# Graph layers on one core: chunks of target blocks cut as sixteen of three and one of one

## The chip, the cores and the metric

The kernel runs on one core of one Trainium2 chip. The metric is the device time of one execution in microseconds (us); the median of three runs stands for a kernel.

## What is computed

Four graph networks stand one behind another, on 6250 nodes with 128 features and 100000 edges, with a residual sum and a layer norm behind each. The first two are attention networks. The work that the change touches is the last two, which sum over neighbours, cut here to what matters:

```python
# third network: four graph convolutions (self-loops, degree norm)
h = relu(gcn_conv(x, edges, W1, b1)); h = relu(gcn_conv(h, edges, W2, b2))
h = relu(gcn_conv(h, edges, W3, b3)); h = relu(gcn_conv(h, edges, W4, b4))
x = layernorm(x + h)
# fourth network: two GIN convolutions on the same edges
def gin_conv(x, src, dst, Wa, ba, Wb, bb):
    h = x + segment_sum(x[src], dst)
    return relu(h @ Wa + ba) @ Wb + bb
h = relu(gin_conv(x, ..., W1a, b1a, W1b, b1b))     # 128 -> 256 -> 256
h = relu(gin_conv(h, ..., W2a, b2a, W2b, b2b))     # 256 -> 256 -> 128
x = layernorm(x + h)
```

## The kernel before

Nodes are padded to 49 blocks of 128. An earlier phase counts the edges between every pair of blocks into a dense matrix of bytes in HBM (`adjacency`). The phase `dense` (L2084) then computes a graph layer as a matrix product: the features of 49 source blocks, each split into a high and a low part that add up to it (`parts`, type fp32r), are the stationary operands, and the counts of a chunk of target blocks are the moving operand.

The phase runs seven units (`UNITS`): three of kind `gcn`, one `gcn_end`, and `gin`, `gin_left` and `gin_right` (the second GIN layer takes its 256 features in two halves). The function `chunks` (L2016) cuts the 49 target blocks of a unit into 17 chunks of up to three blocks (`TRIO`). Each pair of unit and chunk is an item, 7 x 17 = 119 in all. A chunk of n blocks is n*128 columns wide.

Within an item the 49 source blocks go by in 17 groups k of three (the last group has one). For each group one engine turns the bytes of the chunk into fp32r numbers in one of four buffers `moving`: the string `SHARES` says which, seven times GpSimd (L2229), six times ScalarE (L2350), four times VectorE (L2495). TensorE then issues two matmuls for each source block of the group (L2288), each with a weight load of its own, so 98 matmuls in an item whatever the width of the chunk, all adding up in one bank of PSUM. A cast may run up to four groups ahead of TensorE (it waits for `eaten` of the group four before).

What is to be done with an item's sums, its steps, is written into the next item: the functions `step` of TensorE (L2233), ScalarE (L2307) and VectorE (L2400) issue the steps of item g-1 at fixed groups k of item g. For `gcn` these are the product with the norm at k = 0, the relu at k = 2, the product with the next weights on TensorE at k = 4 (L2240), the product with the norm at k = 7, and the split into parts for the next layer (VectorE cuts and subtracts at k = 7 and 8, ScalarE copies at k = 10). `gcn_end` has transposes at k = 4 (L2245), row statistics at k = 7, the normalization, the cut and the low part at k = 12 and 13, the high part at k = 14. `gin` and `gin_right` have the hidden product at k = 2 (L2252, L2254, L2255) and the output product at k = 8 (L2263). The last item's steps come behind its matmuls with nothing beside them.

In the first item of a unit TensorE waits at each group for the parts of the chunk that holds the group's last source block (`holding`, L2124).

The counts of an item come by one DMA on SyncE's queue into one of two buffers (`load`, L2153). The load of item g waits until all casts of item g-2 are done. In program order SyncE goes through load(g), load_norm(g), store(g-3), load_x(g). VectorE's `fill(g+1)` (L2356) waits, behind k = 11 of item g, for the counts of item g+1 to land and adds the self-loops; all casts of item g+1 wait for that, and so do VectorE's own later steps and its cast k = 15 of item g, which stand behind it.

Of the kernel before, what the change touches and what calls it, by code (L numbers as in the profile page):

```python
# [24 lines left out]
P = 128  # L25
NODES, EDGES, D = 6250, 100000, 128
BLOCKS = -(-NODES // P)
# [369 lines left out]
def wait(engine, sem, n):  # L397

    if not (isinstance(n, int) and n <= 0):
        engine.wait_ge(sem, n)  # L400
# [1603 lines left out]
TRIO = 3  # L2004
# [10 lines left out]

def chunks():  # L2016

    pairs = -BLOCKS % TRIO
    sizes = [TRIO] * ((BLOCKS - 2 * pairs) // TRIO) + [2] * pairs
    assert sum(sizes) == BLOCKS  # L2020
    return [(sum(sizes[:k]), n) for k, n in enumerate(sizes)]


CUTS = len(chunks())
ITEMS = [(u, kind, b, n) for u, kind in enumerate(("first",) + UNITS) for b, n in chunks()]
SIGNALS = {"first": "cut high low",
           "gcn": "scaled relued projected rowed cut high low",
# [12 lines left out]
def upto(name, e):  # L2040

    return COUNT_TO[name, e] if e >= 0 else 0
# [41 lines left out]
def dense(nc, m, d, t, tables, adj, out):  # L2084
# [14 lines left out]
    with Phase(nc, "de", names) as (  # L2099
# [9 lines left out]
        def item(g):  # L2109
            u, kind, b, n = ITEMS[g + CUTS]  # L2110
            return u - 1, kind, b, n, g + CUTS
# [12 lines left out]
        def holding(block):  # L2124

            return [e for e, (b, n) in enumerate(chunks()) if b <= block < b + n][0]
# [8 lines left out]
        def normed(kind):  # L2135
            return kind in ("gcn", "gcn_end")
# [14 lines left out]
        @block.sync  # L2151
        def _(sp):
            def load(g):  # L2153
                u, kind, b, n, e = item(g)
                wait(sp, by_act, (g - 1) * SHARE["a"])
                wait(sp, by_dve, (g - 1) * SHARE["d"])
                wait(sp, by_pool, (g - 1) * SHARE["p"])
                sp.dma_start(d.counts[g % 2][:, 0:n * SLOTS * WIDE].rearrange("p (b w) -> p b w", b=n),
                             adj[b * P:(b + n) * P, :].rearrange("(b p) w -> p b w", p=P)).then_inc(counts_in[g % 2], 16)

            def load_norm(g):
                u, kind, b, n, e = item(g)
                if normed(kind):
                    wait(sp, scaled, upto("scaled", e - 2))
                    sp.dma_start(d.norm_row[g % 2][:, 0:n * P],
                                 tables["norm"].rearrange("(o b) p -> o (b p)", o=1)[:, b * P:(b + n) * P].broadcast_to([P, n * P])
                                 ).then_inc(norm_in[g % 2], 16)

            def load_x(g):
                u, kind, b, n, e = item(g)  # L2170
                if kind in ("gcn_end", "gin_right"):
                    wait(sp, rowed if kind == "gcn_end" else rested, upto("rowed" if kind == "gcn_end" else "rested", e - 2))
                    if kind == "gin_right":
                        sp.wait_ge(stored, 16 * CUTS)
                    sp.dma_start(d.x_in[g % 2][:, 0:n * P].rearrange("p (b f) -> p b f", f=P),
                                 tables["x1" if kind == "gcn_end" else "x"][b * P:(b + n) * P, :].rearrange("(b p) f -> p b f", p=P)
                                 ).then_inc(x_in[g % 2], 16)

            def store(g):
                if g < 0:  # L2180
                    return
                u, kind, b, n, e = item(g)
                if kind == "gcn_end":
                    sp.wait_ge(lned, upto("lned", e))
                    sp.dma_start(tables["x"][b * P:(b + n) * P, :].rearrange("(b p) f -> p b f", p=P),
                                 d.h[:, 0:n * P].rearrange("p (b f) -> p b f", f=P)).then_inc(stored, 16)
                if kind == "gin_right":
                    sp.wait_ge(lned, upto("lned", e))
                    whole_blocks = n if (b + n) * P <= NODES else n - 1
                    last = sp.dma_start(out[b * P:(b + whole_blocks) * P, :].rearrange("(b p) f -> p b f", p=P),  # L2190
                                        d.h[:, 0:whole_blocks * P].rearrange("p (b f) -> p b f", f=P)).then_inc(stored, 16)
                    if whole_blocks < n:
                        sp.dma_start(out[(b + n - 1) * P:NODES, :], d.h[0:LAST, (n - 1) * P:n * P]).then_inc(stored, 16)

            load(0)
            load(1)
            for k, name in enumerate(("g2", "g3", "g4")):
                r, c = t[name].shape
                sp.wait_ge(padded, 3)
                sp.dma_start(d.g[k][0:r, 0:c], t[name]).then_inc(params_in, 16)  # L2200
            sp.dma_start(d.w1a[:, :], t["w1a"]).then_inc(params_in, 16)
            for to, name in ((d.w1b, "w1b"), (d.w2a, "w2a"), (d.w2b, "w2b")):
                sp.dma_start(to, t[name].rearrange("(k p) n -> p k n", p=P)).then_inc(params_in, 16)
            spread_at = {name: sum(n for _, n in SPREAD[:k]) for k, (name, _) in enumerate(SPREAD)}
            for to, name, n in ((d.b1b, "b1b", 2 * D), (d.b2b, "b2b", D)):
                sp.dma_start(to[:, :], t["spread"][:, spread_at[name]:spread_at[name] + n].broadcast_to([P, n])).then_inc(params_in, 16)
            sp.wait_ge(norm_copied, 1)
            sp.dma_start(tables["norm"], d.a[0:BLOCKS, 0:P]).then_inc(norm_out, 16)
            sp.wait_ge(norm_out, 16)
            sp.wait_ge(low, upto("low", 1))  # L2210
            for g in range(total):
                if g >= 2:
                    load(g)
                load_norm(g)
                store(g - 3)
                load_x(g)
            for g in range(total - 3, total):
                store(g)
            sp.wait_ge(stored, 16 * (2 * CUTS + 1))

        @block.gpsimd
        def _(pool):
# [628 lines left out]
```

## Time and profile before

| | us |
|---|---|
| median of three runs | 5488.98 (5485.43 to 5491.85) |
| the profiled execution | 5493.95 |
| its span | 5492.1 |
| the dense phase in it | 3311.0 to 5492.1, of which TensorE is busy 2140.6 |

The granted TensorE clock over the whole span is 0.88 of full speed on average, 1.0 in nearly all of the dense phase. The profile's times are those of one execution, with what was busy on each engine, which wait ended the idle time before an instruction, and a chain of work followed back from the end. Matmuls overlap one another, so the price of one is read from the distance between starts in an undisturbed row, not from its duration.

### The profile page before, as it was taken

How to read it: one execution, taken by the hardware profiler on the slowest of the kernel's cores; microseconds unless marked ns; L12 is line 12 of the kernel's file. 1: busy time of each engine (PE TensorE's matmuls, PEld its weight loads, DVE VectorE, ACT ScalarE, POOL GpSimd, SP SyncE). 2: the span in 40 equal slices, each digit the busy share in tenths (PEclk: the TensorE clock that was granted, in tenths of full speed). 3: DMA queues.
4: the chain of work that ended last, by engine and by line, in shares of the span. 5: the costliest groups of instructions: out<-in, count | busy, mean ns of one | idle time of the engine just before them, and what ended most of it. 6: DMA issues, size and time to landing. Idle time of an engine off the chain costs nothing. (4 is left out here: it accounts for less than half of the span.)

```text
span 5492.1 us, 99934 instructions
## 1 busy us (share of the span) xinstructions
PE 4376.5 (80%) x24072; PEld 3667.3 (67%) x24073; DVE 3581.9 (65%) x7941; ACT 2266.5 (41%) x4134; POOL 2777.4 (51%) x2730
## 2 busy tenths in 40 slices
PE   7566667666567777777648848999999999999998
PEld 4455555554234444444347738999999999999998
DVE  4888888886478888888786675444445654443444
ACT  0333443332135555555426644444444443344333
POOL 0477777773047777777412103444444443344433
PEclk8788888887887777877779959999999999999999
DMA  1444444442157777777425534343434442233332
GB/s 46 121 117 117 118 117 116 117 116 81 33 168 198 198 200 197 199 198 198 136 65 158 154 84 163 141 151 143 149 141 161 173 151 106 101 135 144 138 125 94
DMA packets 543152, 750.77 MB, mean 137 GB/s; under 512 B 57967, under 2 KB 441966, under 8 KB 542734
## 3 DMA queue, kind: packets, MB, share of 16 engines
q1 hardware_dynamic: 461182, 521.35, 28.4%
q0 software_dynamic: 81552, 224.63, 15.4%
q8 instruction: 166, 2.72, 0.2%
q14 instruction: 252, 2.06, 0.1%
HBM read 584.36 MB, written 161.41 MB: 136 GB/s over the span
## 5 line engine op out<-in xcount | busy, mean ns | idle before, releaser
L544 POOL DMA_INDIRECT arena<-table_kv,arena x1664 | 1732.7, 1041 | 653.1 <-issue 505.2
L2288 PE MATMUL ps<-moving,parts 128*128 128x384 f32 (+1 forms) x11662 | 2015.8, 331 | 38.5 <-ACT moving L2350 20.4
L2288 PEld LDWEIGHTS ps<-moving,parts 128*128 128x128 f32 x11662 | 1949.5, 188 | 72.1 <-ACT moving L2350 29.3
L2229 POOL CAST moving<-counts 128x1152 fp32r<-128x1152 uint8 (+1 forms) x420 | 476.2, 1134 | 737.9 <-PE ps L2288 606.4
L340 ACT ACTIVATE counted<-ps 128x392 uint8<-128x392 f32 x1568 | 665.0, 503 | 333.7 <-PE ps L331 300.3
L2229 POOL CAST moving<-big 128x1152 fp32r<-128x1152 uint8 (+1 forms) x413 | 468.6, 1135 | 610.1 <-PE ps L2288 610.1
L331 PE MATMUL ps<-by_place,by_lo 128*128 128x392 bf16 x1568 | 631.2, 525 | 105.3 <-DVE by_place L295 74.2
L654 PE MATMUL ps<-arena 128*128 128x137 f32 x1664 | 321.3, 349 | 344.6 <-DVE arena L788 332.5
L2350 ACT ACTIVATE moving<-counts 128x1152 fp32r<-128x1152 uint8 (+1 forms) x360 | 366.9, 1024 | 436.0 <-PE ps L2288 433.0
L2350 ACT ACTIVATE moving<-big 128x1152 fp32r<-128x1152 uint8 (+1 forms) x354 | 360.4, 1023 | 429.7 <-PE ps L2288 429.6
L654 PEld LDWEIGHTS ps<-arena 128*128 128x128 f32 x1664 | 273.1, 239 | 374.0 <-ACT arena L699 222.5
L2495 DVE CAST moving<-counts 128x1152 fp32r<-128x1152 uint8 (+1 forms) x240 | 312.7, 1303 | 287.7 <-PE ps L2288 287.6
L2495 DVE CAST moving<-big 128x1152 fp32r<-128x1152 uint8 (+1 forms) x236 | 307.4, 1302 | 289.7 <-PE ps L2288 289.7
L562 PEld LDWEIGHTS ps<-arena 128*128 128x128 bf16 x1680 | 140.7, 122 | 519.2 <-DVE arena L556 437.0
L321 DVE TENSOR_TENSOR slots<-slots,counted 128x196 uint16 x1568 | 405.7, 259 | 96.8 <-DVE slots L321 48.1
L562 PE MATMUL ps<-arena 128*128 128x128 bf16 x1680 | 197.3, 249 | 268.7 <-DVE arena L556 262.4
L295 DVE TENSOR_TENSOR by_place<-count_fours,count_place 128x1568 bf16<-128x1568 f16 (+1 forms) x497 | 395.2, 795 | 0.0
L331 PEld LDWEIGHTS ps<-by_place,by_lo 128*128 128x128 bf16 x1568 | 187.9, 124 | 254.7 <-issue 183.8
L883 PE MATMUL ps<-big,arena 128*128 x1672 | 323.3, 356 | 0.4 <-ACT arena L909 0.4
L883 PEld LDWEIGHTS ps<-big,arena 128*128 128x128 f32 x1672 | 300.7, 263 | 27.2 <-issue 18.5
L666 PE MATMUL ps<-big,arena 128*128 x1680 | 289.4, 330 | 0.4 <-ACT arena L694 0.4
L704 ACT ACTIVATE arena<-arena 128x32 f32<-128x32 f32 x208 | 48.3, 232 | 582.6 <-DVE arena L781 582.6
(329 smaller groups left out, 5337.3 us busy)
## 6 DMA issues: line engine op xcount, KB each, us to landing
counts<-adjacency SPq DMA_DIRECT2D x53, 2352.0 KB, 8.5
big<-adjacency SPq DMA_DIRECT2D x52, 2352.0 KB, 8.6
adjacency<-slots SPq DMA_DIRECT2D x784, 98.0 KB
edge_values<-arena SPq DMA_DIRECT2D x208, 256.0 KB
arena<-edge_values SPq DMA_DIRECT2D x208, 256.0 KB, 3.3
arena<-table_kv,arena POOLq DMA_INDIRECT x1664
big<-table_norm SPq DMA_DIRECT2D x60, 192.0 KB, 5.7
big<-adjacency SPq DMA_DIRECT2D x7, 1568.0 KB, 6.6
```

What stands on the lines that cost most here:

```text
L295: return dve.tensor_tensor(ct.by_place[:, r % 2, n], ct.fours[:, n], copies(ct.place[:, ds(c * HALF, HALF)], 1, last - first), ALU.is_equal)
L321: dve.tensor_tensor(ct.slot_pairs[:, ds(to[k], WIDE // 2)], ct.slot_pairs[:, ds(of[k], WIDE // 2)], ct.counted_pairs[:, r % 2, k, :], ALU. ...
L331: pe.matmul(m.bank(bank, WIDE), ct.by_lo[:, r % 2, :, k], ct.by_place[:, r % 2, :, k], start=True, stop=True).then_inc(ct.product, 1)
L340: act.activation(ct.counted[:, r % 2, k, :], m.bank(bank, WIDE), ACT.Copy).then_inc(ct.moved, 1)
L544: pool.indirect_dma_start(m.ring4[r][:, k * 2 * D:(k + 1) * 2 * D], None, table, bass.IndirectOffsetOnAxis(m.src[:, j * HALF + k:j * HALF ...
L562: mm = pe.matmul(bank[:, k * P:(k + 1) * P], m.hit16[:, r, :, k], m.ident16, start=True, stop=True)
L654: mm = pe.matmul(summed(k), m.hit[:, r % 2, k, :], m.msg[:, r % 2, k, :], start=True, stop=True)
L883: mm = pe.matmul(m.bank(6 + h)[:, k * P:(k + 1) * P], m.hitT[:, h, k, :], m.q[:, ds(at[k] * D, D)], start=True, stop=True)
L2229: pool.tensor_copy(to, of).then_inc(by_pool, 1)
L2288: mm = pe.matmul(m.bank(g % 2, n * P), d.parts[SOURCE[u]][:, s + q, t_, :], moving[:, q * n * P:(q + 1) * n * P], start=(s + q == 0 and t_ ...
L2350: act.activation(to, of, ACT.Copy).then_inc(by_act, 1)
L2495: dve.tensor_copy(to, of).then_inc(by_dve, 1)
```

## The change

`chunks` gives sixteen chunks of three blocks and one of one in place of fifteen of three and two of two. The number of chunks stays 17. Two places follow from it: in `gin_right` the last chunk has only the last, partial block, so its store of whole blocks falls away and only the store of the 106 remaining rows is left; the wait at the end counts one transfer fewer.

```diff
 def chunks():
 
-    pairs = -BLOCKS % TRIO
-    sizes = [TRIO] * ((BLOCKS - 2 * pairs) // TRIO) + [2] * pairs
+    sizes = [TRIO] * (BLOCKS // TRIO) + [BLOCKS % TRIO]
     assert sum(sizes) == BLOCKS
     return [(sum(sizes[:k]), n) for k, n in enumerate(sizes)]
...
                     whole_blocks = n if (b + n) * P <= NODES else n - 1
-                    last = sp.dma_start(out[b * P:(b + whole_blocks) * P, :].rearrange("(b p) f -> p b f", p=P),
-                                        d.h[:, 0:whole_blocks * P].rearrange("p (b f) -> p b f", f=P)).then_inc(stored, 16)
+                    if whole_blocks > 0:
+                        sp.dma_start(out[b * P:(b + whole_blocks) * P, :].rearrange("(b p) f -> p b f", p=P),
+                                     d.h[:, 0:whole_blocks * P].rearrange("p (b f) -> p b f", f=P)).then_inc(stored, 16)
                     if whole_blocks < n:
                         sp.dma_start(out[(b + n - 1) * P:NODES, :], d.h[0:LAST, (n - 1) * P:n * P]).then_inc(stored, 16)
...
-            sp.wait_ge(stored, 16 * (2 * CUTS + 1))
+            sp.wait_ge(stored, 16 * 2 * CUTS)
```

## Rows read from the trace of the kernel before

**Rows 1.** The page: busy time, and the granted TensorE clock in 40 slices.
```profile
PE 4376.5 (80%) x24072; PEld 3667.3 (67%) x24073; DVE 3581.9 (65%) x7941; ACT 2266.5 (41%) x4134; POOL 2777.4 (51%) x2730
...
PEclk8788888887887777877779959999999999999999
```

**Rows 2.** Busy time in two of the units; the last line sums all seven.
```profile
core 0: us, PE busy (x) PEld busy (x) DVE busy (x) ACT busy (x) POOL busy (x), PEclk, DMA share, GB/s
3611.30:3903.00 291.70, 291.62 (x1766) 289.19 (x1765) 133.03 (x186) 121.97 (x137) 136.98 (x119) 1.00 0.40 147
...
4837.70:5120.80 283.10, 281.48 (x1681) 280.56 (x1680) 115.64 (x156) 119.78 (x140) 132.49 (x119) 1.00 0.39 141
...
sum 2181.10, PE 2140.61 PEld 2085.48 DVE 1036.46 ACT 876.15 POOL 943.49; mean PE 305.80 PEld 297.93 DVE 148.07 ACT 125.16 POOL 134.78
```

**Rows 3.** Chain that ended last: an undisturbed run in three-block items, one in two-block items.
```profile
4659.24 6.24 PE ps L2288 x36
...
4810.45 4.31 PE ps L2288 x36
```

**Rows 4.** TensorE in order of time at half clock: start, us, what, count; then the clock, and durations in ns.
```profile
3254.62 1.06 PE L1376 MATMUL ps<-ident,arena 128*128 128x128 f32 x4
3256.69 3.31 PE L1828 MATMUL ps<-w,arena 128*128 128x100 f32 x14 [1.01 <-ACT arena L1817]
...
3260.00:3268.00 8.00, 1.75 (x7) 1.35 (x7) 7.76 (x13) 3.72 (x9) 0.00 (x0) 0.50 0.32 91
...
L1828 PE MATMUL ps<-w,arena x98: 421/421/534, 3222.7 to 3292.4; 128*128 128x100 f32 x98
```

**Rows 5.** Lines L2288, L2240, L2245: count, duration in ns min/median/max, first and last start.
```profile
L2288 PEld LDWEIGHTS ps<-moving,parts x11662: 186/188/333, 3311.0 to 5476.6; 128*128 128x128 f32 x198
...
L2240 PEld LDWEIGHTS ps<-dense_g,dense_b x294: 187/192/192, 3342.2 to 4201.5; 128*128 128x128 f32 x147
L2240 PE MATMUL ps<-dense_g,dense_b x294: 272/275/275, 3342.3 to 4201.6; 128*128 128x128 f32 x147
...
L2245 PEld LDWEIGHTS ps<-ident,dense_b x49: 138/141/145, 4218.6 to 4489.6; 128*128 128x128 f32 x49
```

**Rows 6.** TensorE in order of time at full clock: one step's six records.
```profile
3573.68 0.83 PE L2240 MATMUL ps<-dense_g,dense_b 128*128 128x128 f32 x6
```

**Rows 7.** Casts by width: busy us, mean ns.
```profile
L2229 POOL CAST moving<-counts 128x1152 fp32r<-128x1152 uint8 x370 | 434.3, 1174 | 553.4 <-PE ps L2288 551.9 <-DVE big L2363 1.5
...
L2350 ACT ACTIVATE moving<-counts 128x384 fp32r<-128x384 uint8 x53 | 27.8, 524 | 79.5 <-PE ps L2288 79.5
```

**Rows 8.** End of `gcn_end` in order of time: TensorE, SyncE's queue, VectorE, TensorE.
```profile
4461.72 0.49 PE L2245 MATMUL ps<-ident,dense_b 128*128 128x128 f32 x3
4474.00 0.38 PE L2245 MATMUL ps<-ident,dense_b 128*128 128x128 f32 x2
...
4455.08 0.39 SPq L2158 DMA_DIRECT2D big<-adjacency  x1
4469.15 0.38 SPq L2158 DMA_DIRECT2D counts<-adjacency  x1
...
4465.23 1.34 DVE L2396 TENSOR_SCALAR dense_h<-big,dense_two,dense_inverse 128x128 f32<-128x128 f32 x3
4478.71 1.32 DVE L2363 TENSOR_TENSOR counts<-counts,dense_one 128x128 uint8<-128x128 uint8 x3 [1.91 <-DMA counts<-adjacency]
...
4481.11 1.25 DVE L2376 TENSOR_TENSOR parts<-dense_h,dense_cut 128x256 fp32r<-128x256 f32 x1
...
4483.28 6.47 PE L2288 MATMUL ps<-moving,parts 128*128 128x256 f32 x38 [1.71 <-DVE moving L2495]
```

**Rows 9.** Chain that ended last, behind the last matmul over the counts.
```profile
5477.05 0.39 ACT dense_a L2316
...
5477.48 0.70 PE ps L2254 x2
...
5480.15 1.14 PE ps L2263 x8
```

## The prediction

> **What bounds the kernel now.** I read the page first: TensorE is the busiest engine, and in the last 16 or so of the 40 slices its clock is full and it is busy nine tenths or more [rows 1]. Those slices are the dense phase, the only part the change touches. A table of busy time cut at the starts of its seven units shows how tight it is: in a `gcn` unit TensorE is busy 291.62 of 291.70 us, in `gin_left` 281.48 of 283.10, in all 2140.61 of 2181.10, while VectorE, ScalarE and GpSimd are each busy less than half [rows 2]. So a unit's time is the number of its matmuls times the distance between their starts, and the question is what that distance is for each width of chunk. Casts, steps and loads matter only where one of them comes late.
>
> The chain that ended last gives the two prices known. An undisturbed run of 36 matmuls lasts 6.24 us in a three-block item (384 columns) and 4.31 us in a two-block item (256 columns) [rows 3]: 0.1733 and 0.1197 us each. For one block (128 columns) there is no row.
>
> **Part 1, the matmuls.** An item issues 98 matmuls at any width, and there are 17 items in a unit before and after. So the change takes two items of 98 at 0.1197 us out of each unit and puts in 98 at 0.1733 and 98 at an unknown price p:
>
> per unit 98 x (0.1733 + p - 2 x 0.1197) = 98 x (p - 0.0661) us.
>
> The bounds of p: if columns alone count, p lies on the line through the two known prices, 0.1197 - (0.1733 - 0.1197) = 0.0661, and the change costs exactly nothing here. If a narrower matmul saves nothing, p = 0.1197 and a unit costs 98 x 0.0536 = 5.25 us more.
>
> What could keep p off the line is the weight load, since each matmul brings its own 128 columns of weights and these don't get narrower. Two rows at half clock (0.50) speak to this: four f32 records with 128 moving columns take 1.06 us, and fourteen with 100 moving columns 3.31 us [rows 4]. Take off the last one's duration (0.421 us for L1828 [rows 4]; I take the same for L1376) and divide by the remaining 3 and 13: 0.213 and 0.222 us. With 22% fewer columns the distance doesn't fall at all; so something that doesn't depend on the moving columns sets it, and the weights are the same 128 columns in both. At full clock that floor would be half, 0.107 to 0.111. At full clock six records with 128 moving columns take 0.83 us, of which the last one's 0.275 is its tail: (0.83 - 0.275) / 5 = 0.111 [rows 5, 6].
>
> Does the floor hold for L2288, whose type is fp32r and not f32? By duration its weight loads are the same kind: 188 ns median against 192 for the f32 loads of L2240, while the load in front of a transpose (L2245) takes 141 [rows 5]. I take p = 0.111, because the nearest row in width, clock and duration of the weight load gives that. Then a unit costs 98 x (0.111 - 0.0661) = 4.40 us more, seven units **30.8 us**.
>
> Here the Trainium skill states two rules that part company. TensorE: Matmul & The Clock Gate, section LDWEIGHTS (loading the stationary operand), gives a load P / 1.2 ns, 107 ns for 128 columns, whatever is moved; by that figure the estimate would be 98 x 7 x (0.107 - 0.0661) = 28 us. Its section Back-to-back issue gap gives N / 2.4 + 2.5 ns, so 56 ns at 128 columns; by that rule the change would be free, since the same columns and the same number of matmuls are issued. The rows at 384 and 256 columns lie 11 ns above the second rule, and the rows at half clock follow the first.
>
> **Part 2, the steps on TensorE.** The steps of a three-block and a one-block chunk together issue the same number of records per block, or the same columns, as those of two two-block chunks. The six records of L2240 belong to one three-block chunk, two a block [rows 6]. Cost nothing; no cover is needed, the work is the same.
>
> **Part 3, the casts.** In a one-block item a group lasts 6 x 0.111 = 0.67 us at the forecast price, against 0.72 in a two-block item. Casts shrink more: GpSimd takes 1.174 us for 1152 elements, and ScalarE's one-block casts of 384 take 0.524 [rows 7]; I take 0.55 for 384 on any engine. The busiest, GpSimd, has seven casts in an item: 3.9 of 10.9 us. TensorE covers them. Without that cover (p on the line, a group of 0.40 us) GpSimd would still need only 3.9 of 6.5 us. Cost nothing, or a few tenths per unit where a step sits in front of a cast.
>
> **Part 4, the load behind the short item.** The next unit's first chunk is loaded while the last, short item runs. At the end of `gcn_end` this is late today [rows 8]: SyncE issues the load at 4469.15; VectorE, stopped in `fill` behind k = 11, goes on at 4478.71, 9.56 us later; fill, normalization, cut and low part stand in front of its cast k = 15, and TensorE idles 1.71 us for that cast. Reckoned from the start of the last item (30 matmuls before the transposes at 4474.00, so about 4470.3) the load goes out at -1.1. After a three-block item it goes out earlier: the one at 4455.08 came 3 us before the start of its next item (30 matmuls before 4461.72, about 4458.0). So the counts land at about -3 + 9.6 = +6.6; then fill 1.3, the normalization of three blocks 1.34 with some wait, cut 0.4, low part 1.25 and the cast 0.55 give +11.6. TensorE reaches group 15 at 90 x 0.111 + 0.5 = +10.5. It waits 1.1 in place of 1.7: **-0.6 us**. In the other units only fill and the cast stand there, done at about +8.5, before TensorE reaches group 15 at 10.0 or later. If the price were on the line TensorE would be there at +6 to +7 and this cover gone: waits of about 1.7 us in each `gcn` unit, 5 in place of 1.7 in `gcn_end`, 1 in `gin`, 2.5 in `gin_left`, together some 12 us more than now.
>
> On SyncE's queue nothing else moves: behind the load stand load_norm, store and load_x of the same items as before, whose data are needed an item later.
>
> **Part 5, the end and the boundary.** Behind the last matmul the span runs from 5477.05 to 5492.1, bare. Its chain is ScalarE's copy, eight records of the hidden product, the relu, eight records of L2263 [rows 9] and VectorE's row work, on two blocks. With one block, the hidden product (2.0 us from 5477.48) and L2263 (1.14) halve, -1.5; the copy, the relu and the row operations lose about 0.1 each, -0.7; one of two stores falls away, -0.2. **-2.4 us**, between -1.5 and -3. At the start of a unit, group 15 no longer needs the last chunk's parts, only group 16 does. But TensorE is idle for 0.08 us in all of the second `gcn` unit [rows 2], so no such wait exists there to be saved: worth nothing, or 0.5 in the other units.
>
> **Sum:** 30.8 - 0.6 - 2.4 = +27.8 us. On the profiled execution (span 5492.1, 1.85 around it, 5493.95) that gives 5522; this execution lies 5 us above the median of 5488.98. On the median: **5517 us**, +0.5%.
>
> **The rivals.**
> 1. *Column price, late load.* p = 0.0661, the matmuls cost nothing more, but the loads of part 4 come late: +12 - 2.4 = +10, 5499. For it: two of three widths lie on a line. Against it: the half-clock rows.
> 2. *Not slower.* p = 0.0661 and the load lands in time (its 9.56 us includes contention that the smaller chunk might ease): the one mechanism left is the bare tail, -2.4, 5487. Its place is the last 15 us; it decides as soon as 7 x 98 x (p - 0.0661) is under 2.4 us, p below 0.070. The section on the issue gap named above would give this. Against it: the same rows, and the DMA row.
> 3. *The narrow form falls to the rate of plain f32*, where a product takes two records (294 records for 147 products in three units [rows 5, 6]): p = 2 x 0.111 = 0.222, 7 x 98 x (0.222 - 0.0661) = 107, less 3: 5593. Nothing in the trace shows an fp32r matmul under 256 columns, so it can't be excluded; nothing speaks for it.
> 4. *Full weight-load price and more.* p = 0.1197 by the row of the next wider form: 36.8 - 3 = +34, 5523; with a few tenths per unit where a three-block chunk's steps now stand beside a short item, 5527.
>
> **How the numbers follow.** Forecast with its own range 5508 to 5528 (p from 0.100 to 0.1197, rival 4 among it): 80%. Rival 1: 8%. Rival 2: 5%. Rival 3: 7%. The range 5498 to 5529 holds the forecast, rival 4 and rival 1, and leaves out rivals 2 and 3. Faster by over 0.2% (11 us, about what a measurement of this kernel can tell from no change) would need p under the time of the columns themselves: 1%. Within 0.2%: rivals 1 and 2 nearly whole, 12%. Slower: 87%.
>
> **What would show it.** In `gin_left`, which has no TensorE steps, the last item should last about 10.9 us (6.5 on the line, 11.7 at the two-block price, 21.8 in rival 3), and the one before it 17.0. The weight loads should keep their 188 ns. At the end of `gcn_end` VectorE should wait for the DMA and TensorE for L2495 by about a microsecond. The tail should lose 2 to 3 us. A narrow run of 36 matmuls under 3 us would fell the forecast.

## The result and the profile after

The changed kernel takes 5511.19 us against 5488.34, medians of five runs each: the ratio is 1.0043 with a 95% interval of 1.0028 to 1.0058. Run a second time beside fifteen runs of the kernel before, it gave 5513.73 against 5491.72, a ratio of 1.0042 (1.0028 to 1.0056). The forecast was 5517, +27.8 us; the medians say +22.9 and +22.0.

The dense phase says it more sharply, since the phases ahead of it, which the change doesn't touch, take 3292 to 3311 us in the profiled executions. Busy time in the seven units of the changed kernel, columns as in [rows 2]:

```profile
3301.20:3605.80 304.60, 300.22 (x1762) 296.53 (x1763) 145.76 (x223) 126.62 (x147) 138.73 (x119) 0.99 0.39 141
3605.80:3901.70 295.90, 295.90 (x1767) 293.71 (x1766) 130.98 (x186) 122.00 (x137) 137.19 (x119) 1.00 0.39 145
3901.70:4198.90 297.20, 296.25 (x1769) 294.06 (x1767) 131.97 (x189) 122.00 (x137) 137.21 (x119) 1.00 0.39 145
4198.90:4489.50 290.60, 290.60 (x1718) 287.80 (x1718) 186.87 (x345) 126.56 (x153) 132.39 (x119) 1.00 0.47 167
4489.50:4848.50 359.00, 349.77 (x1925) 331.50 (x1925) 150.91 (x189) 138.00 (x185) 133.46 (x119) 1.00 0.30 111
4848.50:5134.60 286.10, 284.66 (x1677) 283.93 (x1676) 114.79 (x156) 119.58 (x140) 132.58 (x119) 1.00 0.38 139
5134.60:5508.30 373.70, 353.80 (x2000) 329.17 (x1998) 169.20 (x329) 121.68 (x155) 133.18 (x118) 0.99 0.33 116
sum 2207.10, PE 2171.20 PEld 2116.68 DVE 1030.48 ACT 876.43 POOL 944.74; mean PE 310.17 PEld 302.38 DVE 147.21 ACT 125.20 POOL 134.96
```

The second unit is still all matmuls, 295.90 of 295.90 us; it had 291.62 in 291.70 [rows 2]. The sum went from 2181.1 to 2207.1, **+26.0 us**, and TensorE's busy time from 2140.6 to 2171.2: the loss is matmuls that start further apart, not waiting. By units, from the starts of their first matmuls:

| unit | before | after | change | forecast |
|---|---|---|---|---|
| gcn, gcn, gcn | 300.3, 291.7, 293.0 | 304.6, 295.9, 297.2 | +4.3, +4.2, +4.2 | +4.4 each |
| gcn_end | 288.3 | 290.6 | +2.3 | +3.8 |
| gin, gin_left | 353.4, 283.1 | 359.0, 286.1 | +5.6, +3.0 | +4.4 each |
| gin_right with the end | 371.3 | 373.7 | +2.4 | +2.0 |

(`gin` and `gin_left` are to be read as a pair: the steps of the last chunk of `gin` run in the first item of `gin_left`, and a one-block chunk has fewer of them.)

The last item of `gin_left`, which has no other work on TensorE, in the changed kernel (columns as in [rows 2]):

```profile
5123.70:5134.60 10.90, 10.90 (x100) 10.90 (x98) 3.52 (x10) 3.63 (x7) 4.30 (x7) 1.00 0.60 218
```

98 matmuls of one block in 10.89 us from first start to first start, the granted clock full: 0.1111 us each. The forecast said 10.9. The durations of L2288 in the changed kernel, as in [rows 5]:

```profile
L2288 PEld LDWEIGHTS ps<-moving,parts x11662: 185/188/338, 3301.2 to 5495.9; 128*128 128x128 f32 x198
L2288 PE MATMUL ps<-moving,parts x11662: 220/335/660, 3301.2 to 5495.9; 128*128 128x384 f32 x186, 128*128 128x128 f32 x12
```

The weight loads last 188 ns in the median as before, the shortest matmul 220 ns where it was 277.

### The profile page after: what moved, and what is told of

It is laid out like the page before. It is cut to its first block and busy times, and to the rows that moved or that the text cites. A ratio compares the mean times of both kernels' runs of the same rounds, so it can differ in the third digit from the quotient of the medians.

```text
span 5508.3 us, 99933 instructions
## 1 busy us (share of the span) xinstructions
PE 4400.0 (80%) x24072; PEld 3691.2 (67%) x24073; DVE 3576.0 (65%) x7941; ACT 2266.2 (41%) x4134; POOL 2777.6 (50%) x2730
## 5 line engine op out<-in xcount | busy, mean ns | idle before, releaser
L2288 PE MATMUL ps<-moving,parts 128*128 128x384 f32 (+1 forms) x11662 | 2046.1, 335 | 35.5 <-ACT moving L2350 19.9
L2288 PEld LDWEIGHTS ps<-moving,parts 128*128 128x128 f32 x11662 | 1980.5, 189 | 68.3 <-ACT moving L2350 28.9
L666 PE MATMUL ps<-big,arena 128*128 x1680 | 293.0, 333 | 0.4 <-ACT arena L694 0.4
```

What stands on the lines that cost most here:

```text
L2288: mm = pe.matmul(m.bank(g % 2, n * P), d.parts[SOURCE[u]][:, s + q, t_, :], moving[:, q * n * P:(q + 1) * n * P], start=(s + q == 0 and t_ ...
```

## The experiments

**Half the moved columns.** If the weights set the distance, moving less still must win nothing.

```diff
+                            few = P // 2 if n == 1 and u > 0 else n * P
-                            mm = pe.matmul(m.bank(g % 2, n * P), d.parts[SOURCE[u]][:, s + q, t_, :],
-                                           moving[:, q * n * P:(q + 1) * n * P],
+                            mm = pe.matmul(m.bank(g % 2, few), d.parts[SOURCE[u]][:, s + q, t_, :],
+                                           moving[:, q * n * P:q * n * P + few],
```

> The changed kernel, but in the one-block items of units two to seven each matmul over the counts moves 64 of its 128 columns, and loads all its weights; so the sums of half of the last block are left out. If the weight load sets the distance between the starts of narrow matmuls (0.111 us), nothing gets shorter: the last item of gin_left stays at 10.9 us, the dense phase within 1 us of the changed kernel's 2207.1. If the moved columns still count (0.0536 us per 128 of them), that item falls by 98 x 0.0268 = 2.6 us to 8.3, and the dense phase by 6 x 2.6 = 16 us to 2191. If a narrow fp32r matmul is slowed the more the narrower it is, the item grows.

Measured: the dense phase takes 2249.8 us, 42.7 more than the changed kernel's, and the last item of `gin_left` 17.4 us in place of 10.9. Only the third reading has the item grow, and not for the reason that the trace shows. Three stretches of 3 us in that item and one in the next, columns as in [rows 2] (the clock is third from the right; a stretch counts also the two or so matmuls under way at its left edge):

```profile
5155.60:5158.60 3.00, 3.00 (x29) 3.00 (x28) 0.55 (x1) 0.74 (x3) 1.19 (x3) 1.00 1.02 426
5160.00:5163.00 3.00, 3.00 (x16) 3.00 (x16) 1.15 (x4) 0.52 (x1) 0.00 (x0) 0.50 0.22 70
5167.00:5170.00 3.00, 3.00 (x16) 3.00 (x15) 0.98 (x3) 0.31 (x1) 0.31 (x1) 0.50 0.23 31
5173.00:5176.00 3.00, 3.00 (x12) 3.00 (x11) 0.57 (x1) 1.16 (x1) 0.83 (x1) 0.54 1.01 422
```

In the first stretch the clock is full and the starts are 0.112 us apart: halving the columns won nothing, as the weight load wants. Then the granted clock fell from 2.4 to 1.2 GHz, and the starts are 0.213 us apart, the same 0.213 to 0.222 that the half-clock rows gave for f32 [rows 4]. So the expectation of 10.9 us failed by the clock, and the weight load as what sets the distance is borne out in the part of the item at full clock.

**Half the weights.** The other half of the test: the moved columns stay, the weight load shrinks.

```diff
+                            few = P // 2 if n == 1 and u > 0 else P
-                            mm = pe.matmul(m.bank(g % 2, n * P), d.parts[SOURCE[u]][:, s + q, t_, :],
+                            mm = pe.matmul(m.bank(g % 2, n * P)[0:few, :], d.parts[SOURCE[u]][:, s + q, t_, 0:few],
```

> The changed kernel, but in the one-block items of units two to seven each matmul loads 64 of its 128 columns of weights and moves all its 128 columns; so half of the features of the last block are left out. If the weight load sets the distance, it halves to about 0.055 us and the line of the columns takes over, 0.066: the last item of gin_left has 6.5 us of matmuls, and now the load of the next unit's first chunk comes late: TensorE should wait for VectorE's cast behind its fill, some 2.5 us in gin_left and 1 to 2 in gcn, 3 to 4 in gcn_end; the item ends at 8.5 to 9.5 us in place of 10.9, and the dense phase is some 15 to 20 us shorter than the changed kernel's 2207.1. If the floor is the moving operand's or the issue's, the item stays at 10.9 and the dense phase at 2207.

Measured: the last item of `gin_left` 7.95 us (10.89), of the second and third `gcn` 8.55 and 8.56 (11.60), of `gcn_end` 11.96 (11.44); the dense phase 2193.2, 13.9 us shorter. The last item of `gin_left`, columns as in [rows 2], then the end of it on VectorE and TensorE in order of time:

```profile
5124.90:5132.80 7.90, 6.28 (x100) 5.96 (x97) 3.58 (x8) 3.95 (x7) 4.27 (x8) 1.00 0.71 285
```
```profile
5130.76 0.69 DVE L2364 TENSOR_TENSOR counts<-counts,dense_one 128x128 uint8<-128x128 uint8 x3 [2.56 <-DMA counts<-adjacency]
```
```profile
5131.97 0.69 PE L2289 MATMUL ps<-moving,parts 128*64 128x128 f32 x8 [1.48 <-DVE moving L2496]
```

TensorE is busy 6.28 us of 7.90 and stands 1.48 us for the cast behind the fill, which itself waited 2.56 us for the counts. With half the weights (the shortest weight load of this run lasts 132 ns, that of the changed kernel 185) the matmuls start 0.060 us apart, a little under the line of the columns (0.066), and the late load of rival 1 steps forward, as part 4 said that it would. A floor from the moved columns or from issue would have left 10.9. In `gcn_end` TensorE waits so long for the cast behind the fill and the split that the item gets longer, and the clock is at half behind that wait:

```profile
4491.11 8.30 PE L2289 MATMUL ps<-moving,parts 128*64 128x128 f32 x38 [3.97 <-DVE moving L2496]
```
```profile
4492.00:4496.30 4.30, 4.30 (x17) 4.30 (x16) 1.55 (x2) 1.57 (x2) 1.21 (x2) 0.50 0.96 327
```

(The first row runs on into the next item.) That item, the first of `gin`, takes 19.15 us in place of 17.22. Without these 1.9 us the whole would be about 16 (an estimate), inside the 15 to 20 expected, and not 13.9.

**The price by itself.** The kernel before, with `gin_left` turned into a scale, each item with another number of weight columns and moved columns:

```diff
+TRIED = [(128, 384), (128, 320), (128, 256), (128, 224), (128, 192), (128, 160), (128, 128), (128, 96), (128, 64),
+         (96, 128), (64, 384), (64, 256), (64, 192), (64, 128), (128, 384), (64, 256), (64, 256)]
+                held, moved = TRIED[g % CUTS] if kind == "gin_left" else (P, n * P)
-                            mm = pe.matmul(m.bank(g % 2, n * P), d.parts[SOURCE[u]][:, s + q, t_, :],
-                                           moving[:, q * n * P:(q + 1) * n * P],
+                            mm = pe.matmul(m.bank(g % 2, moved)[0:held, :], d.parts[SOURCE[u]][:, s + q, t_, 0:held],
+                                           moving[:, q * n * P:q * n * P + moved],
```

> The kernel before, but in the unit gin_left, which has no steps on TensorE, the matmuls of each item hold another number of weight columns and move another number of columns (the sums of that unit are so left out in part). It measures the disputed price by itself. If the price is the larger of the column line (0.0125 + columns / 2.4 ns) and the weight load (0.107 to 0.112 us at 128 weight columns): with 128 weight columns 0.173 at 384 moved, 0.146 at 320, 0.120 at 256, then 0.111 at 224, 192, 160, 128, 96 and 64. With 64 weight columns 0.173 at 384 still, 0.120 at 256, 0.093 at 192 and 0.066 at 128. With 96 weight columns and 128 moved about 0.083. If the 0.0125 us above the columns belong to the weight load, the items with 64 weight columns come out lower than 0.173 and 0.120. If a narrow fp32r matmul has a rate of its own, there is a step at 256 moved columns and a slope below it. Items of less than about 10 us wait for casts and loads; the price is then read within a group.

Median distance between the starts of an item's matmuls, in us, from the trace:

| weight columns | 384 moved | 320 | 256 | 224 | 192 | 160 | 128 | 96 | 64 |
|---|---|---|---|---|---|---|---|---|---|
| 128 | 0.173 | 0.147 | 0.120 | 0.113 | 0.111 | 0.112 | 0.112 | 0.213 (half clock) | 0.213 (half clock) |
| 96 | | | | | | | 0.160 (half clock) | | |
| 64 | 0.174 | | 0.113 | | 0.089 | | 0.060 | | |

Six of the items in the table of busy time (columns as in [rows 2]): 256, 128, 96 and 64 moved with all weights, 128 moved with 96 columns of weights, 256 moved with 64 of them:

```profile
4873.10:4884.80 11.70, 11.70 (x100) 11.70 (x99) 8.35 (x9) 6.81 (x9) 8.21 (x7) 1.00 0.53 197
...
4920.00:4931.30 11.30, 11.23 (x100) 11.05 (x99) 7.89 (x9) 6.83 (x8) 8.11 (x7) 1.00 0.59 215
4931.30:4949.40 18.10, 17.93 (x101) 17.80 (x99) 7.29 (x11) 7.53 (x10) 8.04 (x7) 0.61 0.49 170
4949.40:4970.30 20.90, 20.90 (x100) 20.90 (x99) 6.86 (x10) 7.27 (x9) 8.03 (x7) 0.50 0.32 119
4970.30:4986.00 15.70, 15.70 (x100) 15.70 (x101) 6.70 (x10) 6.79 (x9) 8.15 (x7) 0.50 0.35 128
...
5056.40:5067.50 11.10, 11.10 (x99) 11.10 (x98) 4.70 (x9) 5.05 (x8) 5.89 (x7) 1.00 0.33 118
```

With 128 weight columns the distance falls with the columns down to about 224 and is flat from there: the floor is 0.111 to 0.113. There is no step at 256 and no rate of its own for narrow fp32r, so rival 3 is out. At 96 and 64 the floor is the same at full clock (the first starts of the 96-column item are 0.111 to 0.112 apart; for 64 see the first experiment) and 0.213 at half clock. The item with 96 weight columns ran wholly at half clock: 0.160, three quarters of 0.213, as 96 is of 128. So at one clock and with the floor in force, the distance goes with the columns of weights, while fewer moved columns change nothing. With 64 weight columns the floor is gone, 0.060 at 128 moved. The 0.0125 us above the columns shrink with the weights at 256 (0.120 to 0.113), and not at 384, where most of the item's distances are at full clock; whose they are stays open.

**A two-block chunk first.** To part the late load from the widths, the kernel before with its chunks in another order:

```diff
-    pairs = -BLOCKS % TRIO
-    sizes = [TRIO] * ((BLOCKS - 2 * pairs) // TRIO) + [2] * pairs
+    sizes = [2] + [TRIO] * ((BLOCKS - 4) // TRIO) + [2]
...
-            sp.wait_ge(low, upto("low", 1))
+            sp.wait_ge(low, upto("low", 2))
```

(The second line moves a wait at the start by one chunk.)

> The kernel before with one of its two two-block chunks put first: chunks of 2, fifteen of 3, and 2. The matmuls are the same; only the item ahead of the last one is now a three-block item, as in the changed kernel. If the 1.71 us that TensorE waits at the end of gcn_end comes from the load that is issued late behind a two-block item, the load now goes out about 1.6 us earlier against the start of the last item and the wait vanishes or falls under 0.5: dense phase 2181.1 - 1.7 = 2179.4, and gcn_end's last item 12.4 in place of 14.1. If it comes from VectorE's work on the chunk ahead (now three blocks, not two), the wait stays or grows to 2 or 3 us. The end behind the last matmul stays at 15 us.

Measured: dense phase 2179.3, last item of `gcn_end` 12.39. The end of `gcn_end` in order of time, SyncE's queue, VectorE, TensorE:

```profile
4462.58 0.38 SPq L2157 DMA_DIRECT2D counts<-adjacency  x1
```
```profile
4472.12 0.49 DVE L2362 TENSOR_TENSOR counts<-counts,dense_one 128x128 uint8<-128x128 uint8 x2
4472.52 0.17 DVE L2392 RECIPROCAL dense_inverse<-dense_root 128x3 f32<-128x3 f32 x1
4472.73 1.34 DVE L2395 TENSOR_SCALAR dense_h<-big,dense_two,dense_inverse 128x128 f32<-128x128 f32 x3
```
```profile
4469.22 0.49 PE L2244 MATMUL ps<-ident,dense_b 128*128 128x128 f32 x3
4469.46 10.81 PE L2287 MATMUL ps<-moving,parts 128*128 128x256 f32 x86
```

The fill no longer waits for the DMA, and TensorE runs through without a gap where it stood 1.71 us [rows 8]. So VectorE's work on a three-block chunk is not what made TensorE wait, and the late load is. Its start is not parted here from its size: the load goes out 2.7 us before the start of the last item in place of 1.1, but the unit's first chunk now has two blocks, so the load, the fill and the cast behind it are smaller too. The changed kernel loads three blocks at the same 2.7 us ahead, and has no such wait either (below).

**The single chunk first.** The same matmuls as the changed kernel, with a three-block chunk at the end:

```diff
-    pairs = -BLOCKS % TRIO
-    sizes = [TRIO] * ((BLOCKS - 2 * pairs) // TRIO) + [2] * pairs
+    sizes = [BLOCKS % TRIO] + [TRIO] * (BLOCKS // TRIO)
```

(with the same wait moved as above)

> Chunks of one and sixteen of three, the single one first: the same matmuls as the changed kernel, in another order. By the theory that the matmuls carry the loss and the bare end gives a part back, the distance in the one-block item stays at 0.111 us, and the end behind the last matmul, now on three blocks, grows from 12 to about 18 us; the first unit's first item, which waits for its parts to be made, loses about 1 us more. Dense phase 2207.1 + 6 + 1 = 2214. If the end did not depend on the width, it would stay near 2207.

Measured: 2210.6, +3.5 against the changed kernel and not +7. The first item of `gin_right`, which has no steps on TensorE, takes 10.89 us, again 0.111 a matmul. The end grew: from ScalarE's copy at 5490.51 to the span's end at 5507.5 it takes 17.0 us, 5 more than the changed kernel's. Its chain:

```profile
5490.51 0.50 ACT dense_a L2315
5491.01 0.04 issue
5491.05 0.91 PE ps L2253 x2
...
5494.70 1.59 PE ps L2262 x12
```

What I had left out is that a chunk's steps on TensorE are in the sum once: those of a three-block chunk (about 4.9 us, 21.90 against 16.99 for an item of `gin_right` and one of `gin_left`) that now run bare at the end no longer run inside the unit, and only a one-block chunk's (a third) take their place. So `gin_right` is 375.5 us, 1.8 more than 373.7, where 5.0 - 3.3 = 1.7 would be expected. The first unit's first item, bound by the making of parts, takes 20.9 us where its matmuls need 10.9, and that unit grows by 2.0 (306.65 against 304.63). The other units balance.

**Moving only what stands for nodes.** The scale says that two-block items sit above the floor, at 0.120; the last chunk has only 234 real columns of 256:

```diff
+                            few = (n - 1) * P + LAST if b + n == BLOCKS and u > 0 else n * P
+                            mm = pe.matmul(m.bank(g % 2, few), d.parts[SOURCE[u]][:, s + q, t_, :],
+                                           moving[:, q * n * P:q * n * P + few],
```

> Chunks of 2, fifteen of 3, and 2, as in pair_first, and in units two to seven the last item moves only the 234 columns that stand for nodes (the last block has 106), not 256. By the price curve of the sweep (0.120 us at 256 columns, 0.111 to 0.113 at 224) the distance falls to about 0.112: 6 x 98 x 0.008 = 5 us less than pair_first, a dense phase of about 2174.5 against 2181.1 before, so 6 to 7 us under the kernel before (0.12%). If the weight load set the two-block distance already, nothing would be won and it stays at 2179.

Measured: dense phase 2175.6, 5.5 us under the kernel before, last item of `gin_left` 10.97 in place of 11.75 (0.112 each). Of the 5.5 us the trimming gives 3.7 (2179.3 against 2175.6), where 5 were expected; the order of the chunks gives the rest. The whole time, 5487.66 against 5491.72, has a ratio of 0.9995 (0.9983 to 1.0006), which can't be told from no change. The gain is read from the phase in one profile of each kernel, and two profiles of the changed kernel differ by 1.4 us there.

**The changed kernel again.**

> The changed kernel once more, for the size of the loss: by the dense phase +26 us against before (0.47%); by the first medians +23. Last item of gin_left 10.9 us at full granted clock.

Measured: dense phase 2205.7 (+24.6 against 2181.1) and +22.0 by the medians. The last item of `gin_left`:

```profile
5113.70:5124.60 10.90, 10.90 (x100) 10.90 (x99) 3.23 (x9) 3.56 (x7) 4.27 (x7) 1.00 0.58 215
```

## Why the prediction was right, point by point

- **The price p, 0.111 us.** Right: 0.1111 in the changed kernel. That it is the weight load is shown by three runs together: half the moved columns win nothing at full clock, half the weights bring the distance down to 0.060, and the scale is flat under 224 columns and falls with the columns of weights (0.213 to 0.160 at half clock). The two half-clock rows with 128 and 100 columns [rows 4] had told it already: their starts are both 0.213 us apart, and the 0.222 came from one longer distance, 0.326, at the head of the second row. The first of them is a run of transposes, though, whose weight loads are shorter (230 ns against 333), so it was not quite the pair of like rows that I took it for. The LDWEIGHTS section of the Trainium skill's TensorE: Matmul & The Clock Gate gives 107 ns for 128 columns, and the trace agrees within 5 ns at full clock; at half clock the distance is 213 ns, twice that, so the half-clock rows follow that rule only in not depending on what is moved. The formula that I took from its section Back-to-back issue gap, 56 ns, is called there the gap of an isolated matmul; for a stream with a weight load for each matmul the same section gives about 81 ns at 128 columns. Here it is 111, so neither holds for these matmuls.
- **Steps at nothing.** Right in six units: those of kind `gcn` grew by 4.2 to 4.3 where the matmuls alone say 4.4. Wrong in `gin_right`: the steps of one block more now run inside the unit, since only one block's are left for the bare end and not two, and part 5 counted them as saved. In the chain of the kernel before and of the changed one, the steps in the last item of `gin_right`, the first piece of the hidden product and the whole of L2263:

```profile
5464.57 0.43 PE ps L2254 x2
...
5470.61 0.89 PE ps L2263 x8
```
```profile
5482.73 0.70 PE ps L2254 x2
...
5489.32 1.40 PE ps L2263 x12
```

The hidden product takes 1.73 us before and 2.65 after, so with L2263 the steps there cost 1.4 us more. It is the term that the run with the single chunk first brought to light.

- **Casts at nothing.** Right. Casts of one block took 0.51 us on GpSimd, 0.52 on ScalarE and 0.55 on VectorE, as reckoned.
- **The load behind the short item.** Mechanism right, size off. I left 1.1 us of the wait of 1.71; none is left. In the changed kernel, SyncE's queue and VectorE, then TensorE:

```profile
4475.38 0.39 SPq L2157 DMA_DIRECT2D counts<-adjacency  x1
```
```profile
4485.31 0.69 DVE L2363 TENSOR_TENSOR counts<-counts,dense_one 128x128 uint8<-128x128 uint8 x3 [1.27 <-DMA counts<-adjacency]
4485.92 0.17 DVE L2393 RECIPROCAL dense_inverse<-dense_root 128x3 f32<-128x3 f32 x1
4486.13 0.95 DVE L2396 TENSOR_SCALAR dense_h<-big,dense_two,dense_inverse 128x128 f32<-128x128 f32 x3
4487.11 0.36 DVE L2370 TENSOR_SCALAR dense_cut<-dense_h 128x384 int32<-128x384 int32 x1
4487.50 0.56 DVE L2376 TENSOR_TENSOR parts<-dense_h,dense_cut 128x384 fp32r<-128x384 f32 x1
4487.98 0.55 DVE L2495 CAST moving<-big 128x384 fp32r<-128x384 uint8 x1
```
```profile
4481.42 0.52 PE L2245 MATMUL ps<-ident,dense_b 128*128 128x128 f32 x3
4481.70 10.51 PE L2288 MATMUL ps<-moving,parts 128*128 128x128 f32 x82
```

The load took 9.93 us to the fill, about what I had (9.56); the smaller chunk beside it did not ease it, as rival 2 thought that it might. But from the fill to the end of the cast it is 3.2 us (4485.31 to 4488.53), not the 5.0 I took from rows of before: fill 0.69 where I had 1.3, normalization 0.95 for 1.34, low part 0.56 for 1.25. The long rows of before [rows 8] were the wrong ones to take. GpSimd's casts were running beside several of the long ones, but that this lengthened them was not tried.

- **The end.** Right in kind, -3.0 us in place of -2.4, at the edge of the bounds. The chain in the changed kernel, as in [rows 9]:

```profile
5496.25 0.29 ACT dense_a L2316
5496.54 0.04 issue
5496.58 0.49 PE ps L2254 x2
...
5498.28 0.70 PE ps L2263 x4
```

From 5496.25 to 5508.3 are 12.05 us; before it was 15.05. That L2263 has four records in place of eight is as forecast; hidden product and L2263 together lose 1.3 us (1.5 forecast), and the rest, the row work and the single store, 1.7 where I put down 0.9. Nearly half of what the end loses is not saved but moved into the unit, the 1.4 us above.

With these terms at their measured size the sum is 30.8 - 1.7 - 3.0 + 1.4 = 27.5. The phase says 26.0 in one profile of the changed kernel and 24.6 in the other. So the forecast of 27.8 was right in what carries it, the matmuls, while its small terms were off by 1.1, 0.6 and 1.4 us and happen to balance nearly; the 1.5 to 3 us that are left over were not traced further. Of the rivals, 1 and 2 fall with p, 3 with p and the scale; 4 was 0.0086 us too dear per matmul.

## What to carry to other kernels

Here a matmul that loads 128 columns of weights of its own did not start less than 0.111 us behind the one before, with 224 moved columns or with 64: look for two rows with different widths and the same distance before taking the price from a line through wide ones. Cutting a fixed number of columns into equal pieces is then better than wide ones and a sliver, here by 4.2 us in a `gcn` unit, though the pieces' count is the same. And when the order of pieces is chosen, see what is loaded while the short one runs: a full piece ahead of the last one sends the next load out earlier, and a cut to the valid columns pays only above the floor.

## What I had not expected of the hardware

The granted clock fell while TensorE was busy without a gap by the profile. With 64 columns moved every 0.111 us it went from 1.00 to 0.50 some 3.7 us into the last item of `gin_left` (3 to 9 us into those of other units), and the item took 17.4 us in place of 10.9 (the last items of the other late units took 13.9 to 23.7 in place of 11.4 to 15.4); in the scale it fell in the item with 96 columns (0.61; TensorE had stood 0.17 us there earlier) and stayed at 0.50 through the one with 64. With 128 columns moved at the same distance it stayed at 1.00 through the whole item in the changed kernel, in both of its profiles. After the half-clock items it came back within the next wide one (0.91 on average over 17.5 us). So trimming an item that already sits on the floor, as the one-block chunk with its 106 real columns invites, would have to be tried with an eye on the clock; I did not run that width.
